# First attention of a four-layer kernel: row maxima from key differences, late denominators, value products by two key tiles

## The reference, cut to what matters

```python
q = split_heads(x @ Wq)            # 8 heads of 64, over 2048 rows
k = split_heads(context @ Wk)      # 1601 keys
v = split_heads(context @ Wv)
sim = jnp.einsum('bhid,bhjd->bhij', q, k) * scale
attn = jax.nn.softmax(sim, axis=-1)
out = jnp.einsum('bhij,bhjd->bhid', attn, v)
return out.reshape(...) @ Wo + bo
```

## Time and profile before

| what | value |
|---|---|
| median of 3 runs (lowest, highest) | 2806.76 us (2800.16, 2815.42) |
| profiled execution: time, span | 2817.45 us, 2815.3 us |
| PE busy in the span | 2462.6 us, 87% |
| DVE, ACT, POOL busy | 64%, 43%, 18% |
| mean granted PE clock | 0.912 |
| the 16 blocks of this attention | about 72 to 744 us |

### The profile page before, as it was taken

One profiled execution on the slowest core, in us unless ns is written; L12 is line 12 of the kernel. 1 busy time (PEld: TensorE's weight loads), 2 busy tenths in 40 slices (PEclk: granted clock), 3 DMA queues, 4 the chain that ended last, 5 costly groups with the idle time before them and its releaser, 6 DMA issues.

```text
span 2815.3 us, 32889 instructions
## 1 busy us (share of the span) xinstructions
PE 2462.6 (87%) x12445; PEld 1272.3 (45%) x12476; DVE 1810.2 (64%) x3599; ACT 1197.7 (43%) x1580; POOL 509.9 (18%) x281
## 2 busy tenths in 40 slices
PE   8999998998757884999997999875899999999888
PEld 3222222223322232778664677664444444444277
DVE  5677787887568766234453144374788888887385
ACT  2333433434335430122441122352167766776753
POOL 0333333433222226300001550000000000000011
PEclk8999999999869997999997699987599999999889
DMA  3000000000020004200012220002130202000042
GB/s 117 1 1 1 1 1 1 1 1 1 12 120 1 0 1 152 67 1 1 26 41 90 82 70 1 4 1 62 40 70 3 36 6 32 11 31 1 15 142 85
DMA packets 47865, 93.48 MB, mean 33 GB/s; under 512 B 7211, under 2 KB 32441, under 8 KB 46681
## 3 DMA queue, kind: packets, MB, share of 16 engines
q1 hardware_dynamic: 47078, 90.22, 10.5%
q10 hardware_dynamic: 628, 1.14, 0.2%
HBM read 79.48 MB, written 11.38 MB: 32 GB/s over the span
## 4 chain that ended last, share of the span: by engine, by line
PE 54%; DVE 13%; ACT 3%; issue 2%; DMA 2%; ACTq 0%; SPq 0%; POOL 0%; DVEq 0%; POOLq 0%
PE PS L2378 7%; PE PS L1297 6%; PE PS L2359 4%; DVE pm L2487 4%; PE PS L914 4%; PE PS L2321 4%; PE PS L1255 2%; PE PS L1278 2%; PE PS L1279 2%; PE PS L1280 2%; PE PS L896 1%; PE PS L373 1%; PE PS L1081 1%; DVE xg L324 1%; PE PS L1072 1%
## 5 line engine op out<-in xcount | busy, mean ns | idle before, releaser
L2487 DVE TENSOR_REDUCE pm<-PS 128x1 f32<-128x512 f32 x768 | 478.4, 682 | 92.2 <-PE PS L2321 92.0
L2450 ACT ACTIVATE P<-PS 128x1024 f32<-128x1024 f32 (+1 forms) x416 | 406.5, 1021 | 182.8 <-PE PS L2359 181.2
L682 ACT ACTIVATE P<-PS 128x1024 f32<-128x1024 f32 (+1 forms) x208 | 212.7, 1024 | 322.7 <-PE PS L597 299.8
L2321 PE MATMUL PS<-Ks,Qs 49*128 49x512 f32 x768 | 300.8, 477 | 41.7 <-DMA Qs<-row 24.9
L714 DVE TENSOR_REDUCE pm<-PS 128x1 f32<-128x400 f32 (+1 forms) x512 | 264.8, 562 | 75.8 <-PE PS L563 73.5
L2359 PE MATMUL PS<-Qs,Ks 51*128 51x512 f32 (+1 forms) x832 | 267.3, 438 | 8.6 <-ACT P L2450 8.6
L610 PE MATMUL PS<-P,V 128*64 128x512 f32 (+1 forms) x832 | 227.9, 626 | 4.9 <-ACT P L682 4.9
L2378 PE MATMUL PS<-P,V 128*17 128x512 f32 (+1 forms) x1664 | 224.9, 613 | 0.3 <-ACT P L2450 0.3
L2359 PEld LDWEIGHTS PS<-Qs,Ks 51*128 51x128 f32 (+1 forms) x832 | 135.7, 187 | 193.5 <-ACT P L2450 140.3
L520 POOL TENSOR_TENSOR odd<-odd,P 128x1024 f32<-128x1024 f32 x64 | 164.7, 2573 | 260.4 <-ACT P L682 260.4
L2321 PEld LDWEIGHTS PS<-Ks,Qs 49*128 49x128 f32 x768 | 132.3, 193 | 133.3 <-DVE pm L2487 90.9
(11 more groups left out here) (343 smaller groups left out, 4663.1 us busy)
## 6 DMA issues: line engine op xcount, KB each, us to landing
mi<-in_mask SPq DMA_DIRECT2D x32, 800.5 KB, 4.3
We<-in_L_ffn_w SPq DMA_DIRECT2D x16, 1024.0 KB, 7.2
Wg<-gate_rows SPq DMA_DIRECT2D x8, 1024.0 KB, 11.7
Qs<-q_parts SPq DMA_DIRECT2D x90, 64.0 KB, 3.0
Ks<-k_parts SPq DMA_DIRECT2D x24, 200.1 KB, 6.2
q_parts<-T SPq DMA_DIRECT2D x7, 512.0 KB, 2.8
k_parts<-Tk SPq DMA_DIRECT2D x6, 400.0 KB, 2.6
X<-in_x SPq DMA_DIRECT2D x4, 512.0 KB, 8.3
```

The source lines that it names most:

```text
L682: e.activation(self.P[0:r, n % 4, :, :], PS[0:r, b:b + 2, :], ACT.Exp, scale=0.125).then_inc(*k.ac_exp.up(("A", n)))
L2321: m = e.matmul(PS[:, b, :], self.Qs[rows, s, pr, q0:q0 + 128], self.Ks[rows, s, pr, cs], start=True, stop=not masked)
L2450: e.activation(self.P[0:r, n % 4, :, :], PS[0:r, b:b + 2, :], ACT.Exp, scale=0.25).then_inc(*k.ac_exp.up((3, n)))
L2487: e.tensor_reduce(self.pm[:, u % 2, i, c:c + 1], PS[:, ring.of(("max", key)), :], AX.X, ALU.max).then_inc(*k.dv_max.up((3, *key)))
```

## The change

Maxima. For key positions a = 0..511 and b = 512..1023 the maximum of a pair of scores is score(b) + relu(score(a) - score(b)), and the difference of scores is the score with the difference of keys. So DVE makes `Kd` = Kh[0:512] - Kh[512:1024] once for each head pair. For each query tile and head there are now three products of 512 columns: `over` (with Kd), which ACT reads from PSUM through a relu into the buffer `over` in SBUF; `last` (keys 1024 to 1535), reduced by DVE; `base` (keys 512 to 1023), which DVE adds to `over` and reduces in one instruction, with a second small one that reads the result out. The last 66 keys are the step `rest`: four products of 66 columns in one bank and one reduction for all four query tiles. A block has 24 + 2 such steps instead of 16 pairs, DVE reads 18 times instead of 32 times, and ACT has 8 more instructions of 512 elements.

Each of the 26 steps is for one row half alone and stands in the list beside a score product of the other half, two in each tile. Eight steps are done ahead.

Value products. They stand two tiles together, after the scores of the even tiles, with those of tile 12 after tile 0 of the next block. The DVE and POOL sums stand in the list at the same places as the value products.

Denominators. `den` stands later, and `R` is divided by way of transfers: SP copies one row for each head into `Rc` as 64 x 8, DVE takes one reciprocal of 128 x 8, SP writes it to DRAM and reads it back broadcast into `R`. `norm` and `wo` come later in the block.

Numbers of columns for PE are the same (32 x 400.25 before; 24 x 512 + 8 x 66 now). The core of the diff:

```diff
-        steps = [[(self, "max", (x, qt, c)) for qt in range(4) for c in range(4)] for x in (u, u + 1)]
...
+        return [(self, "max", (u, qt, kind, hh)) for qt in range(4) for kind in ("over", "last", "base")
+                for hh in (1, 0)] + [(self, "rest", (u, hh)) for hh in (1, 0)]
...
-        return [(self, "den", (u,))] + [(self, "recip", (u, i)) for i in range(4)] + [(self, "norm", (u,))]
+        return [(self, "den", (u,)), (self, "recip", (u,))] + [None] * 4 + [(self, "norm", (u,))]
...
-                parts += [(self.divide_steps(u - 1), 0.07, 0.36), (self.project_steps(u - 1), 0.4, 0.65)]
-            if p < 3 and qb < 3:
-                parts.append((self.qk_steps(p + 1)[3 * qb:3 * qb + 3], 0.0, 0.9))
+                parts += [(self.divide_steps(u - 1), 0.2, 0.64), (self.project_steps(u - 1), 0.66, 0.92)]
+            if p < 3 and qb < 2:
+                parts.append((self.qk_steps(p + 1)[4 * qb:4 * qb + 4], 0.0, 0.9))
...
+                product = lambda part, hh: [(self, "score", (u, kt, part, hh))]
+                out += product("Kh", 0) + two[0:1] + product("Kl", 0) + product("Kh", 1) + two[1:2] + product("Kl", 1)
...
+                if kt == 0 and u:
+                    out += [(self, "attend", (u - 1, KT - 1)), (self, "take", (u - 1,)), (self, "sum", (u - 1,))]
+                elif kt and kt % 2 == 0:
+                    out += [(self, "attend", (u, kt - 2)), (self, "attend", (u, kt - 1))]
+                out += later[:1] + slots[2 * kt]
...
+        elif step == "recip":
+            u, = key
+            at.wait_ge(k.ac_misc, ("R", u))
+            for hh in range(2):
+                e.dma_start(self.Rc[64 * hh:64 * hh + 64, :], self.R[64 * hh:64 * hh + 1, :]).then_inc(
+                    *self.ld_den.up((u, hh), 16))
+            at.wait_ge(k.dv_misc, ("recip", u))
+            e.dma_start(self.dd.rearrange("h (p n) -> (h p) n", n=8), self.Rc[:]).then_inc(*self.st_den.up(u, 16))
+            at.wait_ge(self.st_den, u)
+            for hh in range(2):
+                e.dma_start(self.R[64 * hh:64 * hh + 64, :], self.dd[hh:hh + 1, :].to_broadcast([64, 512])).then_inc(
+                    *self.ld_rec.up((u, hh), 16))
...
+            e.activation(self.over[:, n % 3, :], PS[:, ring.of(("max", key)), :], ACT.Relu).then_inc(
+                *self.ac_over.up(key))
...
+                e.tensor_tensor(self.Kd[:, s, :], self.Kh[:, s, 0:512], self.Kh[:, s, 512:1024],
+                                ALU.subtract).then_inc(*k.dv_proj.up(("A", p, "difference")))
...
+                m = e.tensor_tensor_reduce(self.trash[:, n % 2, :], ps, self.over[:, n % 3, :], 1.0, -3.0e38, ALU.add,
+                                           ALU.max, self.pm[:, u % 2, i, 0:1])
+            else:
+                m = e.tensor_reduce(self.pm[:, u % 2, i, 1:2], ps, AX.X, ALU.max)
...
+            e.tensor_reduce(self.pm[:, u % 2, 4 * hh:4 * hh + 4, 2],
+                            PS[:, ring.of(("rest", key)), 0:264].rearrange("p (q n) -> p q n", q=4), AX.X,
+                            ALU.max).then_inc(*k.dv_max.up(("A", *key)))
...
+            e.reciprocal(self.Rc[:], self.Rc[:]).then_inc(*k.dv_misc.up(("recip", u)))
```

More of the change, by code:

```diff
@@ L450, in order @@
         out += weave(([(self, "v", (kt,)) for kt in range(KT)], 0.0, 1.0), (norm0, 0.2, 1.0))
-        out += self.qk_steps(0) + self.max_steps(0)
-        before = None
+        ahead = 8
+        maxima = [s for u in range(16) for s in self.max_steps(u)]
+        out += self.qk_steps(0) + maxima[:26] + self.rows_steps(0) + maxima[26:26 + ahead]
+        done = 26 + ahead
+        later = []
         for u in range(16):
@@ L475, in order @@
-        out += [(self, "attend", before), (self, "take", before[:1]), (self, "sum", before[:1])]
+                parts += [(self.divide_steps(u - 1), 0.2, 0.64), (self.project_steps(u - 1), 0.66, 0.92)]
+            if p < 3 and qb < 2:
+                parts.append((self.qk_steps(p + 1)[4 * qb:4 * qb + 4], 0.0, 0.9))
+            slots = spread(weave(*parts), 25)
+            for kt in range(KT):
+                two = maxima[done:done + 2]
+                done += 2
+                product = lambda part, hh: [(self, "score", (u, kt, part, hh))]
+                out += product("Kh", 0) + two[0:1] + product("Kl", 0) + product("Kh", 1) + two[1:2] + product("Kl", 1)
+                if two and two[1][1] == "rest":
+                    later = self.rows_steps(two[1][2][0])
+                out += slots[2 * kt - 1] if kt else []
+                for part in ("Ql", "mr"):
+                    out += product(part, 0) + product(part, 1)
+                if kt == 0 and u:
[3 more added lines that the diff above has]
+                out += later[:1] + slots[2 * kt]
+                later = later[1:]
@@ L476, in order @@
+        out += [(self, "attend", (15, KT - 1)), (self, "take", (15,)), (self, "sum", (15,))]
         return [s for s in out if s]
@@ L554, in tensor @@
         elif step == "max":
-            u, qt, c = key
+            u, qt, kind, hh = key
             p, s = u // 4, u // 4 % 2
             q0 = u % 4 * 512 + qt * 128
-            k0, kn = CHUNKS[c]
-            for hh in range(2):
-                rows = slice(64 * hh, 64 * hh + 64)
-                b = ring.take(at, ("max", key, hh))
-                at.wait_ge(k.ac_proj, ("A", p, "k", 3))
-                m = e.matmul(PS[:, b, 0:kn], self.Qh[rows, s, q0:q0 + 128], self.Kh[rows, s, k0:k0 + kn], start=True,
-                             stop=True)
+            rows = slice(64 * hh, 64 * hh + 64)
+            b = ring.take(at, ("max", key))
+            if kind == "over":
+                keys = self.Kd[rows, s, :]
+                at.wait_ge(k.dv_proj, ("A", p, "difference"))
+            else:
+                keys = self.Kh[rows, s, (512, 1024)[kind == "last"]:(1024, 1536)[kind == "last"]]
+                at.wait_ge(k.ac_proj, ("A", p, "k", 3))
+            e.matmul(PS[:, b, :], self.Qh[rows, s, q0:q0 + 128], keys, start=True, stop=True).then_inc(
+                *k.pe_max.up(("A", *key)))
+        elif step == "rest":
+            u, hh = key
+            s = u // 4 % 2
+            rows = slice(64 * hh, 64 * hh + 64)
+            b = ring.take(at, ("rest", key))
+            for qt in range(4):
+                q0 = u % 4 * 512 + qt * 128
+                m = e.matmul(PS[:, b, 66 * qt:66 * qt + 66], self.Qh[rows, s, q0:q0 + 128],
+                             self.Kh[rows, s, M - 66:M], start=True, stop=True)
             m.then_inc(*k.pe_max.up(("A", *key)))
@@ L574, in tensor @@
         elif step == "score":
-            u, kt, part = key
+            u, kt, part, hh = key
             s = u // 4 % 2
@@ L668, in scalar @@
             ring.freed["turn", u] = (k.ac_rows, ("A", u))
-        elif step == "score" and key[2] == 1:
-            u, kt, _ = key
+        elif step == "max" and key[2] == "over":
+            u, qt, _, hh = key
+            n = 8 * u + 2 * qt + 1 - hh
+            at.wait_ge(k.pe_max, ("A", *key))
+            if n > 2:
+                v, i = (n - 3) // 8, (n - 3) % 8
+                at.wait_ge(k.dv_max, ("A", v, i // 2, "base", 1 - i % 2))
+            e.activation(self.over[:, n % 3, :], PS[:, ring.of(("max", key)), :], ACT.Relu).then_inc(
+                *self.ac_over.up(key))
+            ring.freed["max", key] = (self.ac_over, key)
+        elif step == "score" and key[2:] == ("mr", 1):
+            u, kt, _, _ = key
             n = 13 * u + kt
@@ L717, in vector @@
         elif step == "rows":
             u, = key
-            at.wait_ge(k.dv_max, ("A", u, 3, 3, 1))
+            at.wait_ge(k.dv_max, ("A", u, 0))
             if u > 1:
```

92 lines of the change are left out of this document (47 added, 45 removed).

## The result

The change makes the kernel faster: 2767.83 us median of 4 runs (2754.6 to 2773.23), beside 2809.03 for the kernel before on the same chip (4 runs, 2800.16 to 2815.42). The ratio is 0.9849, with a 95% interval of 0.9804 to 0.9893. The forecast was 2762, in a range of 2720 to 2806, and faster was the likeliest of the three signs.

A forecast was written before the change was run, and what follows sets the result against it. PE was taken as the bound, with about 53 us of gaps. Blocks gain 44 us, the lead 5, the tail loses 4: 45 off the profiled 2817.45 gives 2772, or 2762 for the median, range 2720 to 2806.

The forecast's parts named there:

- What bounds the kernel: Attention stage: PE is the bound, busy 567 of 620 us, with about 53 us of gaps.
- The two gaps: New PE waits in plain blocks: 1.8 us before tile 6 for tile 4's exponential, 2.1 to 2.6 before the partition sums.
- Rival (a): The two gaps don't appear, since the sum reaches the port before POOL: 2724 us, chance 0.18.
- Couples: Value products two tiles together: PE saves 1.3 us in each of 16 blocks, 21 us "for certain".
- DVE: DVE loses about 8 of 29 us a block: 4 by the reductions, 3.4 by the reciprocals.
- The single placing: A single maximum shares the array with the other half's score product; columns unchanged, 14.0 us a block against 11.2 + 2.7.
- The clock surcharge: Plain blocks: about 2 us added for the lower clock behind two gaps of 2 us each, 35.4 becoming 37.4.
- Rival (b): Waits come back in full, each gap followed by 6.8 us at the lower clock: 2797 us, no change, chance 0.15.
- Rival (c): Slower: later DVE sums lose the port to POOL every time, six a block: 2865 us, chance 0.10.
- Rival (d): Single maxima don't share the array, each costing its own 0.21 us, 87 in all: 2849 us, chance 0.02.
- The ends: Ahead of block 0 the reductions gain 5 us; in the tail the longer reciprocal chain loses 4.
- Blocks 12 to 15: The last four blocks, with the next norm's own waits, gain 5 us.

The follow-up runs named there:

- e9: e4 with value products one tile at a time instead of two together, the sums left in place; 2716.56 us, ratio 0.9706.
- e4: The changed kernel with all DVE sums moved earlier (first, middle and last), each behind its odd tile's maxima or, the last, behind tile 12; 2714.79 us, ratio 0.9678.
- e2: The changed kernel with only a block's first DVE sum moved earlier, from behind tile 4's maxima to behind tile 3's; 2744.4 us, ratio 0.9794.
- e3: The changed kernel with only a block's last DVE sum moved earlier, from behind the next block's first maxima to behind tile 12; 2738.1 us, ratio 0.9763.
- e7: The kernel before with only the value products two tiles together, DVE and POOL sums moving with them; 2816.17 us, ratio 1.0062.
- e1: The changed kernel with value products one tile at a time again, DVE and POOL sums moving with them; 2747.81 us, ratio 0.982.
- e5: The changed kernel with four reciprocals on DVE in place of the round trip through DRAM; 2774.31 us, ratio 0.9911.
- e6: The changed kernel without the relu on ACT and the key differences, DVE alone reducing all three key ranges; 2777.92 us, ratio 0.9925.
- e8: The changed kernel with a tile's two single maxima side by side instead of each beside a score product; 2779.91 us, ratio 0.9921.
- e11: e4 with a tile's two single maxima side by side, as in e8; 2713.52 us, ratio 0.9694.
- e10: e4 with the last block's four reciprocals on DVE instead of the round trip through DRAM; 2706.63 us, ratio 0.9653.

## Why the prediction was right, and where not

**What bounds the kernel** was right, and 2762 is 6 us from the measured 2767.83. But of my 45 us only the 21 of the couples were PE's own work; the rest was to come out of PE's idle time and the clock behind it, and the idle time did not fall: 52.5 us of 620 before, 53.1 of 615 after, since the two new waits (40.4 us) took the place of the old. The gain is in busy time. My 32.0 us of PE's own work in a block was 33.7 before, at a granted clock of 1.00, and my 30.7 was 31.3. Of block 7's 3.9 us the couples are about 1.0 (e9 against e4) and the clock (0.96 to 1.00) about 1.5; the rest isn't settled. It may be that a wait of one row half, while the other works, counted as busy before.

**The two gaps** were named with cause, place and size, and both stand there: 2.04 us before the partition sums (forecast 2.1 to 2.6), 1.70 before tile 6 (forecast 1.8). e2 takes away only the one, e3 only the other. Rival (a), that they don't appear, is out. What it would have been worth shows in e4, where they are removed by hand: ratio 0.9678, with the middle sums moved as well.

**Couples: the term that was mis-sized.** I put them down as 21 us "for certain". Each couple does take 1.87 + 0.09 us, as reckoned. But e9 against e4 gives 11.6, and e7 shows them as a loss on the kernel before. What I summed was PE's own time; a couple also holds back a maximum and a release of P, and part of what PE saves comes back as a wait (0.39 us in e4's block 7, for `norm`). In my sum the gaps stood as a cost of the change as a whole; they were the cost of the couples' late sums, so that couples and late sums together lose (16.8 us in the blocks by e1, 12.1 by e7).

**DVE** came out near: the block holds 24.8 us of DVE instead of 30.8, 6.0 less where I said 8. The new form costs 0.61 us to the next start, read-out included (53.19 to 53.80 in the first pair of the lead, and 0.68 + 0.08 by itself), below my 0.77. e5 and e6 price the two parts of the relief: four reciprocals 20.7 us in the blocks, the relu 11.3. In block 7, at a granted clock of 1.00, it is the other way round, 1.5 and 2.0; e5's blocks hold 51 us at the lower level and e6's 27. I had not split them.

**The single placing** I entered only as "columns stay the same". It is worth 13.5 us (e8) or 10.4 (e11) in the blocks, and 1.9 or 0.9 in block 7 at a granted clock of 1.00, by what it does to banks and to DVE; the working had no term for this.

**The clock surcharge** of 2 us for a plain block was too large. Block 7 has both gaps and a granted clock of 1.00. The stretch of the earlier trace rows that I took as the sign of it does not stand behind a gap of 2 us either: PE's idle times just ahead of 176.60 are 0.39 and 1.14 us. Before, nine stretches at the lower level took 41 us of the stage, after it seven of 3.4 us; of the seven plain blocks among blocks 2 to 12 only two had one. Without the surcharge my plain block is 35.4 us, measured 35.1. The surplus here and the shortfall in the couples partly cancelled. By the table, blocks 1 to 11 gained 7.9 us more than forecast, all the other pieces of the change 12.0 less, and 7.4 came from code that the change does not touch. So that the total came out within 6 us is luck in part; it is more accurate than its terms. Rival (b), which made the clock pay for everything, is out by the same rows.

**Rival (c)**, all later sums lose the port: half true. The sums that begin inside a POOL addition went from 20 of 88 to 39 of 95, 9 of them first sums; but in PE's waits only the first and the last sum of a block show. Their number is not the cost: all DVE sums together take 140.2 us before, 177.3 after and 185.0 in e3, whose blocks are yet 25.6 us shorter than those of after. The point I gave, three sums lost and passed on in a block, was not reached. Rival (d) is out by the timeline at 352.73.

**The ends.** Ahead of block 0 I forecast 5 us. DVE's busy stretch is 13.2 us long, 0.5 over my 12.7, against 18.20, but it starts at 51.98 instead of 49.94, since PE first waits for the key difference, and it holds idle times of 0.70 us:

```profile
51.98 1.29 DVE L776 TENSOR_REDUCE pm<-PS 128x1 f32<-128x512 f32 x2 [0.48 <-PE PS L596]
...
55.19 1.29 DVE L776 TENSOR_REDUCE pm<-PS 128x1 f32<-128x512 f32 x2 [0.70 <-PE PS L596]
```

```profile
50.63 0.39 PE L596 MATMUL PS<-Kd,Qh 64*128 64x512 bf16 x2 [0.29 <-DVE Kd L760]
51.56 1.01 PE L596 MATMUL PS<-Kh,Qh 64*128 64x512 bf16 x3 [0.54 <-DVE Kl L753]
```

So DVE is done 3 us earlier and not 5. The first exponential starts 1.7 us earlier than before (72.4 against 74.1) and the copy behind block 0, for which I had added 2, 1.0; I did not follow where the rest went. The tail lost 5.7 us where I said 4; e10 shows that the transfers are 3.7 of it.

**Blocks 12 to 15** gained 0.7 instead of 5. Waits for POOL and for tile 6 stand there too, and three value products wait for ACT, which has the next norm's work in its queue and waits 5.6 us for DVE in it (L648 in the list of waits, 6.7 us in all, 2.6 the longest); five of the seven stretches at the lower clock fall there. That is read from one trace and was not tested.

## What to carry to other kernels

When two engines share a port, the place of the sharing instruction decides more than its length: find who starts right before it, and put it where its input is first ready, not beside the step whose number it bears. What counts is who waits for the instruction that lost the port, not how many lose it. A term that counts only the bound engine's own saving is an upper bound, not "for certain": ask which releases the new order delays. And a queue's order can matter at 60% load, while a slow transfer can be hidden in the middle of a stage and is paid for at its end.

## What the runs showed of the hardware that was not expected

A DVE sum of two SBUF operands that begins 0.4 us after a POOL addition lasts 3.03 us: POOL had 1.96 left (358.23 + 2.36 - 358.63), and 1.07 of the sum's own 1.2 follow. The two don't share, the one waits, and so it is for all 39 such sums of the stage (1.07 to 1.09 us after POOL's end). Gaps of 2.04 and 1.70 us in block 7 left the granted clock at 1.00, while in block 2 the clock fell to 0.50 at 155.70, within a gap of 2.04 that ended at 155.97, and stayed there for 3.4 us (the stretch shown at the start). The four 66-column products of `rest`, each with its own weights, pass beside one score product of 0.22 us, the lower end of what I allowed; the next product of their own half (at 367.20) starts 0.13 us behind their start (timeline of PE in block 7):

```profile
367.06 0.38 PE L628 MATMUL PS<-Qh,Kh 64*128 64x512 bf16 x1
367.07 0.29 PE L605 MATMUL PS<-Kh,Qh 64*128 64x66 bf16 x4
367.20 0.37 PE L628 MATMUL PS<-Qh,Kh 64*128 64x512 bf16 x1
367.28 0.38 PE L630 MATMUL PS<-Qh,Kl 64*128 64x512 bf16 x1
```

The Trainium skill ("TensorE: Matmul & The Clock Gate", Part 3 on packing small matmuls) lets weight loads overlap running products only where the row group differs; these four stand on the same rows, and the rows show them no slower than a single product of 512 columns. The measurement decides.
